# Layout of q and k in DRAM, joined transfers in the attention steps, and a new order of VectorE's work in the projection

## What is computed

```python
def attention(x, q_w, k_w, v_w, o_w, o_b, unity_scale):      # 16 heads of 16 columns
    q, k, v = heads(x @ q_w), heads(x @ k_w), heads(x @ v_w)
    q = q * sigmoid(unity_scale)
    scores = q @ k.T / sqrt(16)
    allowed = (j % 4 == 0) | (abs(i - j) <= 8)               # i: query, j: key
    out = softmax(where(allowed, scores, -inf)) @ v
    return merged(out) @ o_w + o_b

def linear(x, weight_fp8, bias, input_scale, weight_scale):
    x_q = clip(x / input_scale, -448, 448).astype(float8_e4m3fn)
    return (x_q * input_scale) @ (weight_fp8 * weight_scale).T + bias

return x + attention(xn, ...) + linear(xn, ...)
```

## Time and profile before

| | us |
|---|---|
| Median of 3 runs | 1239.79 (1239.64 to 1245.02) |
| The profiled execution's own time | 1244.37 |
| Its span, first to last instruction | 1242.6 |
| PE busy in the span | 1144.8 (92%) |
| DVE busy | 990.3 (80%) |
| ACT busy | 814.5 (66%) |
| Projection, by the PE's matmuls | up to 243.5 |
| Attention steps, first to last copy of maxima (L935) | 258.4 to 1165.2 |
| Output projection | from 1184.2 |

### The profile page before, as it was taken

One profiled execution on the slowest core, in us unless ns is written; L12 is line 12 of the kernel. 1 busy time (PEld: TensorE's weight loads), 2 busy tenths in 40 slices (PEclk: granted clock), 3 DMA queues, 4 the chain that ended last, 5 costly groups with the idle time before them and its releaser, 6 DMA issues.

```text
span 1242.6 us, 29384 instructions
## 1 busy us (share of the span) xinstructions
PE 1144.8 (92%) x10944; PEld 519.6 (42%) x10944; DVE 990.3 (80%) x1843; ACT 814.5 (66%) x1524; POOL 249.8 (20%) x382
## 2 busy tenths in 40 slices
PE   4899999999999999999999999998989899999999
PEld 2466566523333333333333333333333333333387
DVE  5778888599888889898978988888879788889423
ACT  2343344248777778787777877777878677878800
POOL 2233333301212121212121211112121112121200
PEclk9899999969998889899999999999999899999999
DMA  6566665722222222232222222232223222223168
GB/s 177 140 201 181 205 205 163 210 73 69 62 70 63 74 58 77 57 84 65 73 66 68 72 67 72 60 79 59 76 57 83 64 66 64 74 64 77 55 211 302
DMA packets 178177, 125.68 MB, mean 101 GB/s; under 512 B 43821, under 2 KB 162349, under 8 KB 178029
## 3 DMA queue, kind: packets, MB, share of 16 engines
q1 hardware_dynamic: 173896, 116.98, 34.2%
q10 hardware_dynamic: 4144, 6.88, 1.7%
HBM read 71.47 MB, written 50.99 MB: 99 GB/s over the span
## 4 chain that ended last, share of the span: by engine, by line
PE 56%; SPq 15%; DVE 9%; DMA 7%; issue 6%; ACT 4%; POOL 3%; DVEq 0%; POOLq 0%
PE ps_attend L1136 15%; PE ps_attend L1066 11%; PE ps_attend L1101 7%; SPq L97 5%; DMA q_op<-negmax_rows 5%; PE ps_attend L1216 4%; PE ps_attend L1143 4%; SPq L899 3%; SPq L894 3%; PE ps_project L579 3%; DVE peak_far L1011 3%; PE ps_project L589 3%; ACT probs L942 2%; PE ps_attend L1076 2%; DMA sums<-out_rows 2%
## 5 line engine op out<-in xcount | busy, mean ns | idle before, releaser
L1011 DVE TENSOR_REDUCE peak_far<-ps_attend 128x1 f32<-128x512 f32 x1024 | 631.6, 679 | 14.6 <-PE ps_attend L1101 10.8
L942 ACT ACTIVATE probs<-ps_attend 128x512 f32<-128x512 f32 x1024 | 537.5, 602 | 146.5 <-PE ps_attend L1066 143.2
L1066 PE MATMUL ps_attend<-q_op,k_op 51*128 51x512 f16 x1024 | 284.9, 405 | 39.9 <-DMA q_op<-negmax_rows 33.1
L1136 PE MATMUL ps_attend<-probs,v_op 128*32 128x512 f32 x2048 | 291.3, 643 | 0.0
L1101 PE MATMUL ps_attend<-k_op,q_op 48*128 48x512 f16 x1024 | 243.3, 394 | 23.0 <-DVE peak_far L1011 14.4
L1014 DVE TENSOR_REDUCE peak_near<-ps_attend 128x4 f32<-128x432 f32 x256 | 139.7, 585 | 64.2 <-PE ps_attend L1119 62.6
L1066 PEld LDWEIGHTS ps_attend<-q_op,k_op 51*128 51x128 f16 x1024 | 74.2, 94 | 261.9 <-ACT probs L942 172.8
L947 ACT ACTIVATE probs<-ps_attend 108x512 f32<-108x512 f32 x256 | 138.7, 594 | 39.4 <-PE ps_attend L1079 39.4
L801 POOL CAST negmax<-peak 128x16 bf16<-128x16 f32 x64 | 12.6, 196 | 722.6 <-DVE peak L993 722.6
L1101 PEld LDWEIGHTS ps_attend<-k_op,q_op 48*128 48x128 f16 x1024 | 75.1, 96 | 116.5 <-DVE peak_far L1011 85.3
L792 POOL TENSOR_TENSOR out_rows<-out_rows,share_rows 128x512 f32<-128x512 f32 x64 | 81.4, 1272 | 52.1 <-DMA share_rows<-shares_dram 50.0
(11 more groups left out here) (81 smaller groups left out, 1097.9 us busy)
## 6 DMA issues: line engine op xcount, KB each, us to landing
v_dram<-v_sb SPq DMA_DIRECT2D x64, 256.0 KB, 3.1
v_op<-v_dram SPq DMA_DIRECT2D x48, 288.0 KB
q_op<-q_parts_dram SPq DMA_DIRECT2D x384, 32.0 KB, 2.2
k_op<-k_parts_dram SPq DMA_DIRECT2D x96, 96.0 KB, 2.9
base<-in_x SPq DMA_DIRECT2D x16, 512.0 KB, 4.3
q_parts_dram<-qk_parts SPq DMA_DIRECT2D x32, 256.0 KB, 3.1
share_rows<-shares_dram SPq DMA_DIRECT2D x256, 32.0 KB, 2.3
attn_dram<-out_rows SPq DMA_DIRECT2D x256, 32.0 KB, 1.7
```

The costliest lines, as they stand in the source:

```text
L942: ins = nc.scalar.activation(probs[:, r, h], ps_s[st.bank(kind)], ACT.Exp, scale=undo)
L1011: ins = nc.vector.tensor_reduce(peak_far[:, f, p, tile:tile + 1], bank, AX_X, ALU.max)
L1066: nc.tensor.matmul(bank, k[half(f, KM), keys], q[half(f, KM), p], start=True, stop=True).then_inc(s_ready, 1)
L1136: ins = nc.tensor.matmul(ps_o[h * VW:(h + 1) * VW], v[:, r, h * VW:(h + 1) * VW], probs[:, r, h], start=(r == 0), stop=False)
```

## The change

The stores of q and k write the 48 rows as the array reads them: every part that is used twice is stored twice. DRAM holds for each iteration, pair and half a block [3, 16, 2048], so `load_q` takes two DMAs in place of six and `load_k` eight in place of twelve, each over 48 partitions. A chunk's stores of q and k become twelve DMAs in place of six. In SBUF, k of the two pairs follow each other directly, with padding only at the ends; the far keys now stand after the near ones in each pair. The shares and the attention output move in one DMA each, with the 16 rows of sums between the heads carried along, so `attn_dram` has 128 rows per iteration in place of 64, and the loads of the output projection (`load_heads`) pick 8 blocks of 16 rows. On DVE the deviation and the normalising stand ahead of the float8 rounding and of the low part of k; on ACT the square root (L319) stands ahead of the scaling (L348). The host no longer reorders weight columns, and POOL sets one buffer less.

```diff
 def load_k(...):
-    for f, i in rows:
-        at = f * HALF + i * D
-        to = k_op[at:at + D].rearrange("r (u s) -> r u s", u=PAIRS)
-        src = dram["qk"][1][K_PARTS[i], it].rearrange("(f r u) s -> f r u s", f=2, r=D)[f]
-        eng.dma_start(to[:, :, 0:NS], src[:, :, 0:NS]).then_inc(loaded, 16)
-        eng.dma_start(to[:, :, NS + WPAD:WPAD + S], src[:, :, NS:]).then_inc(loaded, 16)
+    ns = CH // STRIDE
+    for f, u in pairs:
+        rows = dram["k"][it, u, f].rearrange("i r (c s) -> (i r) c s", c=CPB)
+        at = WPAD + u * S
+        eng.dma_start(k_op[half(f), at:at + S - NS].rearrange("r (c s) -> r c s", c=CPB), rows[:, :, ns:]
+                      ).then_inc(loaded, 16)
+        eng.dma_start(k_op[half(f), at + S - NS:at + S].rearrange("r (c s) -> r c s", c=CPB), rows[:, :, 0:ns]
+                      ).then_inc(loaded, 16)
 def load_q(...):
-    for f, i in ROWS:
-        at = f * HALF + i * D
-        src = dram["qk"][0][Q_PARTS[i], it].rearrange("(f r u) s -> f r u s", f=2, r=D)[f]
-        eng.dma_start(q_op[at:at + D, slot], src[:, :, queries * CH:(queries + 1) * CH]).then_inc(loaded, 16)
+    for f in range(2):
+        rows = dram["q"][it, :, f, :, :, queries * CH:(queries + 1) * CH]
+        eng.dma_start(q_op[half(f), slot], rows.rearrange("u i r s -> (i r) u s")).then_inc(loaded, 16)
...
-                    for to, a, e in spans:
-                        sp.dma_start(
-                            pairs[bass.ds(pair, KC), :, to:to + e - a].rearrange("m r s -> r m s"),
-                            qk_parts[:, k, w, part, :, a:e]).then_inc(qk_stored[k], 16)
+                    for m in range(KC):
+                        for i in (Q_ROWS, K_ROWS)[w][part]:
+                            sp.dma_start(
+                                dram["qk"[w]][bass.ds(b4 + m * G // KC, G // KC), :, :, i, :, cq * CH:(cq + 1) * CH
+                                              ].rearrange("g u f r s -> (g u f) r s"),
+                                qk_parts[:, k, w, part, m]).then_inc(qk_stored[k], 16)
...
                 variance(j, n + 2)
+                deviation(j, n + 2)
+                normalise(j, n + 2)
                 fp8_power(j, n + 1)
-                deviation(j, n + 2)
                 if main:
                     low_part(c, k, 1)
-                normalise(j, n + 2)
...
         rows = dram["attn"][bass.ds(b * G + 2 * i, 2), :, n * CH:(n + 1) * CH]
-        eng.dma_start(heads[:, n, i], rows.rearrange("g r s -> (g r) s")).then_inc(heads_loaded[n], 16)
+        eng.dma_start(heads[:, n, i], rows.rearrange("g (h w) s -> (g h) w s", w=VW)[:, 0:D]
+                      ).then_inc(heads_loaded[n], 16)
...
-                for h in range(HG):
-                    sp.dma_start(share_rows[h * VW:h * VW + D], dram["shares"][h].unsqueeze(0).broadcast_to([D, CH])
-                                 ).then_inc(shares_loaded, 16)
+                sp.dma_start(share_rows[:], dram["shares"].unsqueeze(1).broadcast_to([HG, VW, CH])
+                             ).then_inc(shares_loaded, 16)
...
-                for h in range(HG):
-                    sp.dma_start(dram["attn"][st.iteration(-3), h * D:(h + 1) * D, cols],
-                                 out_rows[h * VW:h * VW + D, (st.n - 3) % OUTS]
-                                 ).then_inc(attn_stored[(st.n - 3) % OUTS], 16)
+                sp.dma_start(dram["attn"][st.iteration(-3), :, cols], out_rows[:, (st.n - 3) % OUTS]
+                             ).then_inc(attn_stored[(st.n - 3) % OUTS], 16)
```

More of the change, by code:

```diff
@@ L45 @@
 HALF = P // 2
+PAIRS = HG // 2
 KR = 3 * D
 KM = KR + PARTS
-SK = WPAD + S + WPAD
+SK = WPAD + PAIRS * S + WPAD
+MASK_K = WPAD + S - NS + WPAD
 QSLOTS = 4
-PAIRS = HG // 2
 HI, LO = 0, 1
-K_PARTS = (HI, HI, LO)
-Q_PARTS = (HI, LO, HI)
-ROWS = [(f, i) for f in range(2) for i in range(len(K_PARTS))]
+Q_ROWS = ((0, 2), (1,))
+K_ROWS = ((0, 1), (2,))
 Q_RANGE, K_RANGE, PEAK_RANGE = 2.0 ** 5, 2.0 ** 3, 2.0 ** 13
@@ L79, in half, with load_k @@
     return slice(f * HALF, f * HALF + n)
-def load_k(eng, dram, k_op, loaded, it, rows=ROWS):
-    for f, i in rows:
-        at = f * HALF + i * D
-        to = k_op[at:at + D].rearrange("r (u s) -> r u s", u=PAIRS)
-        src = dram["qk"][1][K_PARTS[i], it].rearrange("(f r u) s -> f r u s", f=2, r=D)[f]
-        eng.dma_start(to[:, :, 0:NS], src[:, :, 0:NS]).then_inc(loaded, 16)
-        eng.dma_start(to[:, :, NS + WPAD:WPAD + S], src[:, :, NS:]).then_inc(loaded, 16)
+def load_k(eng, dram, k_op, loaded, it, pairs=tuple(itertools.product(range(2), range(PAIRS)))):
+    ns = CH // STRIDE
[6 more added lines that the diff above has]
+                      ).then_inc(loaded, 16)
 def load_q(eng, dram, q_op, loaded, it, queries, slot):
-    for f, i in ROWS:
-        at = f * HALF + i * D
-        src = dram["qk"][0][Q_PARTS[i], it].rearrange("(f r u) s -> f r u s", f=2, r=D)[f]
-        eng.dma_start(q_op[at:at + D, slot], src[:, :, queries * CH:(queries + 1) * CH]).then_inc(loaded, 16)
+    for f in range(2):
+        rows = dram["q"][it, :, f, :, :, queries * CH:(queries + 1) * CH]
+        eng.dma_start(q_op[half(f), slot], rows.rearrange("u i r s -> (i r) u s")).then_inc(loaded, 16)
 def part_project(nc, io, dram, keep, ctx):
@@ L248, in body @@
                 b4, cq, k = (j + n // CPB) * G, n % CPB, n % 2
-                pair = (j + n // CPB) * KC
-                ns = CH // STRIDE
                 for w, part in ((0, HI), (0, LO), (1, HI), (None, None), (1, LO)):
@@ L339, in body @@
                     nc.scalar.activation(xnT[:, (n + 1) % 2], ps_t, ACT.Copy).then_inc(xnT_ready, 1)
-                if not main:
-                    deviation(j, n, 2)
+                deviation(j, n, 2)
                 if ahead:
@@ L831, in sync_attend @@
         for k in range(2):
-            sp.wait_ge(done["qk_stored"][k], 16 * 6 * B * CPB // 2)
+            sp.wait_ge(done["qk_stored"][k], 16 * 12 * B * CPB // 2)
             sp.wait_ge(done["v_stored"][k], 16 * TT * B * CPB // 2)
@@ L857, in load_piece @@
             if place < 2:
-                n = 2 * place + piece
-                rows = ROWS[n * len(ROWS) // 4:(n + 1) * len(ROWS) // 4]
-                load_k(sp, dram, k_op[par], k_loaded[par], it, rows)
+                load_k(sp, dram, k_op[par], k_loaded[par], it, [(place, piece)])
             else:
@@ L883, in body @@
                     for k in range(OUTS):
-                        sp.wait_ge(attn_stored[k], 16 * HG * len(range(k, G * CPB, OUTS)))
+                        sp.wait_ge(attn_stored[k], 16 * len(range(k, G * CPB, OUTS)))
                 for i in range(KC):
@@ L958, in scalar_attend @@
         for k in range(2):
-            act.wait_ge(done["qk_stored"][k], 16 * 6 * B * CPB // 2)
+            act.wait_ge(done["qk_stored"][k], 16 * 12 * B * CPB // 2)
             act.wait_ge(done["v_stored"][k], 16 * TT * B * CPB // 2)
@@ L962, in scalar_attend @@
         for k in range(OUTS):
-            act.wait_ge(attn_stored[k], 16 * HG * len(range(k, (B - 1) * G * CPB, OUTS)))
+            act.wait_ge(attn_stored[k], 16 * len(range(k, (B - 1) * G * CPB, OUTS)))
         with act.Fori(1, B - 1) as j:
@@ L972, in scalar_attend @@
                 for k in range(OUTS):
-                    act.wait_ge(attn_stored[k], 16 * HG * len(range(k, STEPS, OUTS)))
+                    act.wait_ge(attn_stored[k], 16 * len(range(k, STEPS, OUTS)))
             for i in range(KC):
@@ L1101, in unit @@
                     nc.tensor.matmul(banks[f], q[half(f), p, tile * P:(tile + 1) * P],
[L1102 removed]
+                                     k[half(f), strided(p):strided(p) + NS], start=True, stop=True).then_inc(u_ready, 1)
                 return
@@ L1262, in build @@
             "q_op": sb("q_op", [P, QSLOTS, PAIRS, CH], F16),
-            "k_op": [sb(f"k_op{i}", [P, PAIRS * SK], F16) for i in range(2)],
+            "k_op": [sb(f"k_op{i}", [P, SK], F16) for i in range(2)],
             "v_op": sb("v_op0", [P, NS // P + S // P, HG * VW]),
-            "mask_k": sb("mask_k", [P, SK - NS], BF16),
+            "mask_k": sb("mask_k", [P, MASK_K], BF16),
             "mask_q": sb("mask_q", [P, S], BF16),
```

53 lines of the change are left out of this document (24 added, 29 removed).

## The result

The changed kernel takes **1153.07 us** (median of 4 runs, 1150.46 to 1155.08), beside 1241.14 of the kernel before in the same comparison: a ratio of 0.9285, 95% interval 0.9252 to 0.9318. The forecast was 1150. Its profiled span is 1153.3 us against 1242.6, at a mean granted clock of 0.978, where the runs of the kernel before had 0.95 to 0.96.

The account below looks back on a forecast made before the run. PE was taken to set the attention step at 12.68 us, with SP's DMA issuing adding some 1.7. Attention -103, projection +5 and output projection +8 sum to -90, giving 1150 us from 1239.8, range 1120 to 1200.

Parts of the forecast that it names:

- Attention, -103: Attention: with SP's DMAs joined, PE sets the step, 12.75 us instead of 14.39 over 63 steps, -103 us.
- SP's 0.6 us for a joined DMA: Attention: each joined DMA of shares or outputs was taken to hold SP's queue 0.6 us.
- The rival by rows: Attention: a DMA holds SP longer with more rows, steps lengthen by some 3 us, +190, 1430 us; chance 0.04.
- VectorE's order: Projection: normalising ahead lets the linear product's add follow at once; gain 0 to 13 us, 12 if PE sets the stage.
- The stores: Projection: q's and k's stores use eight engines, 14.4 us a chunk, covering VectorE's gain; term +5 us.
- Output projection, +8: Output projection: loads of heads use eight engines, 61 us against 48, taken as +8 us (0 to 15).
- Evenly spread: Joined transfers still spread over sixteen engines or changing eights, PE sets the projection: -115, 1125 us; chance 0.15.
- Late sums: Attention: sums on four engines land 0.6 us after DVE wants them, every step grows: +38, 1188 us; chance 0.09.
- The slow eight: Projection and output stage: eight engines run at 16.3 GB/s, 18.1 us a chunk: 1219 us, half of it 1185; chance 0.15.

Follow-up runs that it names:

- e9: e4 with q loaded by six DMAs a step instead of two and the shares by four instead of one: 1181.6 us.
- e10: e4 with q loaded by twelve DMAs a step and the shares by four: 1331.6 us.
- e6: e5 with the projection's operations on VectorE and ScalarE in the order of the kernel before: 1138.8 us.
- e5: The changed kernel with the edits of e1 and e4, and q's and k's stores joined to six a chunk instead of twelve: 1125.6 us.
- e8: The kernel before with only the projection's operations in the changed kernel's order: 1228.9 us, ratio 0.9915.
- e1: The changed kernel with rows ahead of parts in DRAM for q and k, so stores have outer dimension 128 and sixteen engines: 1135.5 us.
- e11: e1 with one unused row behind each block of 16 in DRAM, so a store's outermost dimension is 8 again: 1154.6 us.
- e4: The changed kernel with attn_dram's padding rows removed, four output stores of 16 rows a step, heads loaded as 128 equal rows: 1144.2 us.
- e3: The changed kernel with the four stores of v per chunk issued by ACT's queue: 1157.1 us.
- e12: e1 with the stores of v issued by ACT's queue: 1134.1 us.

## Why the prediction was right

- **Attention, -103.** Measured -102.2 from the second to the last copy, and -96.5 between the ends that the forecast used, the first and the last, because of the long first step. The step's mean is 12.76 us from the second copy on, where I had 12.75: the floor of the earlier trace rows in nearly all, and a few late sums. SP's queue is out of the chain there, and PE's wait for the maxima is down to one. e9 and e10 show the cause: give SP its time back and the long steps return.
- **SP's 0.6 us for a joined DMA.** In the change's steps the shares' load holds SP 0.61 in the median, the store of outputs 0.47 and a load of q 0.59. The rival by rows (1430) is out; its 18 us of SP's time a step were also more than its parts, which give 16.4.
- **VectorE's order, 12 if PE sets the stage.** 13.2 (e6 against e5) and 10.8 (e8). The four instructions of the normalising take 1.6 us a chunk, where I had 1.4.
- **The stores, so that the stage ends at +5.** Measured +5.4 at the second copy, -0.3 at the first copy and +2.3 at the first move of maxima, which is the event that I had reckoned with. Between the change and e1 it is 17.6 us, where my terms make 17. The rule of the count holds: e11 moves the time back with nothing but an unused row. By the Trainium skill, "DMA: Bandwidth & Descriptors", section "Why a DMA increments its semaphore by 16 and not by 1", the outermost dimension decides how many engines serve a DMA; the packet counts of e1, e4 and e11 agree to the last packet. That they are always the same eight, as it has it, no row shows, though e3's longer holds fit it.
- **What the store term left out, and where it was lucky.** I charged SP nothing in this stage, and let the eight engines pace it at 14.4 us a chunk. The runs show SP's queue as the one without free time: an eight-engine store holds it 0.60 instead of 0.33 us at the least. I had the price (0.6) in the attention part and didn't carry it to the 12 stores of a chunk. SP's chunks took 17.9 us for the first, 13.7 in the mean up to the thirteenth, and 20.8, 13.7 and 14.1 at the end, where SP also issues the first loads of k and q. That makes 14.4 in the mean over sixteen, so the term came out right by a sum of other parts, and because both limits lie close together. The last store landed at 257.9 and I had it at 255; the first move of maxima was issued at 261.0 where I had 258. The 5 us more that I gave the first chunks are not seen as such: the 5.4 us at the second copy are this delay and a late landing of the maxima. The rate was taken from the output stage for its packets of 1 KB; its loads of heads are 256 KB over 128 rows, so 2 KB each.
- **Output projection, +8.** Measured +7.5; e4 takes it back (-8.8), with the loads of heads in the chain as foreseen. They also hold ACT's queue 609 ns instead of 359; the chain passes through two of these issues. Part of why it fits is luck too: the last step before it is 2.7 us longer, which the forecast had nowhere.
- **The rivals.** Evenly spread was 1125 us. e5, which makes it true by layout and joins the stores besides, measured 1125.6. Late sums were 1188 us, 38 us over the forecast. They did come late, in six steps, and the load took 3.3 to 4.4 us where this rival had 4.0; but it cost 4.6 us in all, 2.7 of them in the last step, since DVE mostly had time to spare. Why it is longest in the last step isn't shown. The slow eight: the chunks of PE came to 13.4 us in the mean from 163 to 217 us and the last to 16.6, not 18 throughout.

## What to carry to other kernels

Joining DMAs gains where the issuing queue is late, and nothing once its time in the longest step is under the bound engine's (e4 adds 1.5 us a step to SP's time and the steps stay); put the two side by side, in held time and not in number of DMAs, before joining more. Do this in every stage that the DMAs touch. When joining or laying out anew, look at the outermost dimension of both sides: here one that 16 divides kept a store or a load of heads on sixteen engines and nearly halved its hold. If padding or an index gets in between, move it inwards: here that was worth 26 us (e1 and e4), a quarter of what the change brought in the attention.

## What I had not expected of the hardware

- A store of the same 128 KB holds the issuing queue for at least 598 ns on eight engines and 332 on sixteen (e11, e1), a load of 256 KB on ACT 602 and 334 (change, before). The Trainium skill, same section, says that the issuing sequencer itself writes the increments of the engines that a DMA doesn't use; whether this is where the time goes, no run here shows. It can't be all: a load of q over 48 rows, which uses sixteen engines by the count, holds SP 585 ns in the median.
- A queue can be held for longer by what stands behind it: 1.0 us a store in the chunk of e3, and single ones up to 2.16, where the same number of stores over sixteen engines holds it 362 and 402 ns in the median (e12). A long hold is then a symptom, and taking DMAs off that queue gains nothing (e3), while the same edit with sixteen engines costs nothing either (e12). That the eight engines were full in e3 is inferred from this; no row has the share of single engines.
